# Cross-attention loop: maxima turned by VectorE, PSUM banks dealt anew, paired groups of narrow products

## What is computed

```python
x = x + tanh(g[0]) * long_convolution_mix(ctx, ctx, layernorm(x))
x = x + tanh(f[0]) * soft_expert_mix(layernorm(x))
x = x + tanh(g[1]) * L1_xattn(layernorm(x), ctx, ctx)
x = x + tanh(f[1]) * top2_of_8_experts(layernorm(x))

def L1_xattn(q, k, v):                 # b = 16, d = 256, m = n = 512
    h = 8                              # so heads of 32 channels
    qh, kh = q.reshape(b * h, 32, m), k.reshape(b * h, 32, n)
    vh = v.reshape(b * h, 32, n)
    qk = einsum('bdm,bdn->bmn', qh, kh) / sqrt(32)
    return einsum('bmn,bcn->bcm', softmax(qk, -1), vh)
```

## Time and profile before

| | us |
|---|---|
| times of three runs | 1622.12, 1619.13, 1624.82 |
| median | 1622.12 |
| span of the profiled execution (no other time is given for it) | 1622.8 |
| attention: from the first `stir` to the last group of values | 522.4 to 1031.1 |
| second products, first and last start | 543.9, 1028.0 |
| busy over the span: PE, weight loads, DVE, ACT, POOL | 94%, 66%, 73%, 60%, 64% |

### The profile page before, as it was taken

One profiled execution on the slowest core, in us unless ns is written; L12 is line 12 of the kernel. 1 busy time (PEld: TensorE's weight loads), 2 busy tenths in 40 slices (PEclk: granted clock), 3 DMA queues, 4 the chain that ended last, 5 costly groups with the idle time before them and its releaser, 6 DMA issues.

```text
span 1622.8 us, 28609 instructions
## 1 busy us (share of the span) xinstructions
PE 1524.7 (94%) x8929; PEld 1067.6 (66%) x8929; DVE 1189.2 (73%) x1868; ACT 981.3 (60%) x1529; POOL 1031.2 (64%) x855
## 2 busy tenths in 40 slices
PE   4999999998887999999999999888999999999996
PEld 3677777777554644444444444378999998999985
DVE  7788888888827777777777776275777777777774
ACT  6433333334724478888888877746777766766773
POOL 3788888885307588888888887502555555555553
PEclk8999999999998999999999999999999999999998
DMA  7344444445763967777776872581444444444443
GB/s 256 108 131 134 136 142 142 142 132 131 207 176 110 211 163 188 200 187 187 198 190 185 201 188 68 178 303 29 78 78 78 79 78 79 79 78 73 75 77 52
DMA packets 111131, 224.27 MB, mean 138 GB/s; under 512 B 12992, under 2 KB 12992, under 8 KB 110144
## 3 DMA queue, kind: packets, MB, share of 16 engines
q1 hardware_dynamic: 94560, 185.10, 40.3%
q0 software_dynamic: 15904, 37.23, 13.2%
q10 hardware_dynamic: 576, 0.79, 0.2%
HBM read 146.71 MB, written 75.84 MB: 137 GB/s over the span
## 4 chain that ended last, share of the span: by engine, by line
PE 33%; DMA 24%; issue 4%; DVE 4%; ACT 2%; POOL 1%; SPq 0%; ACTq 0%; POOLq 0%; DVEq 0%
DMA out_rows<-XN,slots 22%; PE pB L1471 10%; PE pO L1481 8%; PE pA L1453 7%; PE pO L1494 4%; PE pO L1645 1%; DMA XN<-normed_rows,slots 1%; PE pA L1633 1%; PE pB L1462 1%; PE pA L1549 1%; POOL out_rows L1435 1%; DVE low L1827 1%; DVE XN L2010 0%; DMA qs<-q_low 0%; DVE XN L1944 0%
## 5 line engine op out<-in xcount | busy, mean ns | idle before, releaser
L1827 DVE TENSOR_REDUCE low<-pA 128x2 f32<-128x1024 f32 x256 | 307.0, 1223 | 109.4 <-PE pA L1453 95.8
L1722 ACT ACTIVATE pt<-pB 128x512 f32<-128x512 f32 x512 | 287.7, 594 | 89.7 <-PE pB L1471 81.1
L1435 POOL DMA_INDIRECT out_rows<-XN,slots x71 | 196.9, 2773 | 217.9 <-DMA out_rows<-XN,slots 170.1
L436 PE MATMUL y<-kv,toep 128*128 128x288 f32 x1280 | 326.0, 411 | 9.0 <-DVEq L63 5.8
L436 PEld LDWEIGHTS y<-kv,toep 128*128 128x128 f32 x1280 | 238.0, 190 | 96.8 <-DVEq L63 34.0
L1633 PEld LDWEIGHTS pA<-XN,fc 128*128 128x128 f32 x2272 | 265.6, 192 | 10.9 <-issue 5.6
L1633 PE MATMUL pA<-XN,fc 128*128 128x128 f32 x2272 | 266.4, 276 | 5.0 <-DVE XN L1990 4.0
L1471 PE MATMUL pB<-qs,ks 98*128 98x512 f32 x512 | 226.9, 446 | 3.3 <-ACT pt L1722 2.4
L1471 PEld LDWEIGHTS pB<-qs,ks 98*128 98x128 f32 x512 | 95.6, 188 | 192.2 <-ACT pt L1722 149.2
L406 ACT ACTIVATE ym<-y 128x384 f32<-128x384 f32 (+1 forms) x128 | 52.6, 411 | 228.9 <-PE y L436 228.9
L1787 ACT ACTIVATE proj_high<-WP 128x2048 fp32r x71 | 135.7, 1912 | 83.6 <-PE pO L1645 83.6
(11 more groups left out here) (294 smaller groups left out, 2448.4 us busy)
## 6 DMA issues: line engine op xcount, KB each, us to landing
ks<-ctx_high SPq DMA_DIRECT2D x62, 256.0 KB, 4.6
qs<-q_high SPq DMA_DIRECT2D x62, 256.0 KB, 6.1
kc<-in_ctx_conv SPq DMA_DIRECT2D x32, 384.0 KB, 5.5
XN<-in_x SPq DMA_DIRECT2D x16, 512.0 KB, 9.8
toep<-kernel_and_skip SPq DMA_DIRECT2D x32, 256.0 KB, 3.5
ct<-in_ctx SPq DMA_DIRECT2D x16, 512.0 KB, 6.6
ctx_high<-kh SPq DMA_DIRECT2D x16, 512.0 KB, 4.5
ctx_low<-kl SPq DMA_DIRECT2D x16, 512.0 KB, 5.2
```

Of the source, the lines that this page charges most:

```text
L436: m = pe.matmul(y[half].rearrange("p (l n) c -> p l n c", l=CB)[:, l, :, 0:PAIRS], toep[u][:, (l - s) * P:(l - s + 1) * P], kv[u][:, half, ...
L1435: pool.indirect_dma_start(out=out["out"], out_offset=bass.IndirectOffsetOnAxis(ap=slots[:, j:j + 1], axis=0), in_=ys[j % 2], in_offset=Non ...
L1722: act.activation(pt[s][:, h, :], bank(u, n), ACT.Exp, scale=SCALE1).then_inc(s_exp, 1)
L1827: dve.tensor_reduce(ap(low[u % 2], t % CB * NH + t // CB, [[NH, 2], [1, 1]]), pA[n % 2], op=ALU.max, axis=AX.X, negate=True).then_inc(s_re ...
```

## The change

- **Maxima.** `halves` moves from POOL to DVE, after the last reduction of a unit (in beat 5, for unit `j + 1`), and a third operation there turns 128x32 in blocks of 32x32 into `turned`. `maxima` on PE, `keep` on ACT and the tensor `tops` are gone. `shift` is now four DMAs, one for each 32 queries of a block, each 32 pieces of 128 bytes (4 KB), instead of two of 8 KB in rows of 2 KB.
- **Banks.** `pB` has three banks and a second product waits for the exponential three places before it; `pO` has one, for values alone, so values 0 wait for `att` of the unit before. The sums of unit `j - 1` go into a bank of `pB` as place 7 of 17; the logarithm reads it and is counted with the exponentials, and the second product of beat 9 waits for it.
- **Groups.** Both groups of sums stand together at beat 7, and values 0 and 1 at beat 15; values 2 are at beat 3, values 3 at beat 11.
- **Order.** In beats 3, 6, 7, 8, 10, 11, 13, 14 and 15 the score stands before the second product (before: 2, 5, 10, 13). DVE refines after beat 3, measures after 7, scales after 11. ACT makes the high query after exponential 0, the norm after 4, the logarithm after 6, the inverse after 10, both roots after 15.
- The routing and expert stages get other names for the same number of banks.

```diff
-        low = [sb(st, f"low{i}", [P, CB, NH]) for i in range(2)]
-        split = sb(st, "split", [P, CB, 2 * NH])
+        low = [sb(st, f"low{i}", [P, NH * CB]) for i in range(2)]
+        split = sb(st, "split", [P, 2 * NH * CB])
+        turned = sb(st, "turned6", [P, SQUARE])
-        pB = [pb(st, f"pB{i}", [P, C]) for i in range(2)]
-        pO = [pb(st, f"pO{i}", [P, C]) for i in range(2)]
+        pB = [pb(st, f"pB{i}", [P, C]) for i in range(3)]
+        pO = pb(st, "pO", [P, C])
+        SHIFTS = 16 * P // HD1
+        SUM = 7
-        TURN = 10
+        EARLY_AT = (3, 6, 7, 8, 10, 11, 13, 14, 15)
             def shift(j, u):
-                sp.wait_ge(s_exp, made(j - 1, TURN) if not isinstance(j, int) or j > 0 else 1)
-                for row in range(2):
-                    part = tops[row * NH:(row + 1) * NH]
-                    sp.dma_start(qs[u][NS + row:NS + row + 1], bass.AP(part.tensor, part.offset, [list(part.ap[0]), [C, 1], [1, C]])).then_inc(s_md, 16)
+                sp.wait_ge(s_sp, 3 * j + 3)
+                for n in range(P // HD1):
+                    rows = qs[u][NS:NS + 2].rearrange("r h m -> r (h m)")
+                    sp.dma_start(ap(rows, n * HD1, [[P, NH * CB], [1, HD1]]),
+                                 ap(turned[n * SQUARE:(n + 1) * SQUARE], 0, [[HD1, 1], [1, HD1]])).then_inc(s_md, 16)
             def second(j, u, s, h):
-                n = place(j, s, h)
+                n = place(s, h)
                 if s == 0 and h == 0:
-                    pe.wait_ge(s_md, 32 * j + 32)
-                wait(pe, s_exp, made(j, n - 2))
-                pe.matmul(bank(u, n), ks[u][0:NS + 2, h, s * P:(s + 1) * P].bitcast(F32R), qs[u][0:NS + 2, h, :].bitcast(F32R),
+                    pe.wait_ge(s_md, SHIFTS * j + SHIFTS)
+                if n >= 3:
+                    pe.wait_ge(s_exp, made(j, n - 3))
+                elif exists(j - 1):
+                    pe.wait_ge(s_exp, made(j - 1, TILES - 1 + n % 2))
+                pe.matmul(pB[n % 3], ks[u][0:NS + 2, h, s * P:(s + 1) * P].bitcast(F32R), qs[u][0:NS + 2, h, :].bitcast(F32R),
                           start=True, stop=True).then_inc(s_b, 1)
             def values(j, i, u, s):
                 if s == 0:
                     pe.wait_ge(s_v[u], i * 16 + 16)
-                    wait(pe, s_ln, j)
+                    wait(pe, s_att, j)
+            def sums(j, to):
+                pe.wait_ge(s_add, 4 * j + 4)
+                pe.wait_ge(s_exp, made(j, place(CB - 1, NH - 1)))
+                for rows, last in ((part_sum, False), (pt[CB - 1], True)):
+                    for h in range(NH):
+                        m = pe.matmul(to[h * HD1:(h + 1) * HD1, :], ones, rows[:, h, :], start=not last, stop=last)
+                    m.then_inc(s_sum, 1)
             def body(j, i, u):
                 before = following(j, i, u, -1)
                 for beat in range(TILES):
-                    if beat in (2, 5, 13):
+                    if beat in EARLY_AT:
                         score(*ahead(j, i, u, beat))
-                    if beat == TURN and exists(j + 1):
+                    if beat == SUM and exists(j - 1):
+                        pe.wait_ge(s_exp, made(j, SUM - 3))
+                        sums(j - 1, pB[SUM % 3])
+                    second(j, u, beat // NH, beat % NH)
+                    if beat not in EARLY_AT:
                         score(*ahead(j, i, u, beat))
-                        wait(pe, s_exp, made(j, TURN - 2))
-                        maxima(j + 1, bank(u, TURN))
...
+                    if beat == 3 and exists(j - 1):
+                        values(*before, 2)
+                    if beat == 11 and exists(j - 1):
+                        values(*before, 3)
+                    if beat == 15:
                         values(j, i, u, 0)
-                    if beat == 15:
                         values(j, i, u, 1)
+            def halves(j, u):
+                dve.wait_ge(s_red, DUOS * j + DUOS)
+                dve.tensor_copy(split[:, 0:TILES].bitcast(F32R), low[u % 2]).then_inc(s_sp, 1)
+                dve.wait_ge(s_sp, 3 * j + 1)
+                dve.tensor_tensor(split[:, TILES:].bitcast(F32R), low[u % 2], split[:, 0:TILES], ALU.subtract).then_inc(s_sp, 1)
+                wait(dve, s_md, SHIFTS * j)
+                dve.sem_inc(s_go, 1)
+                dve.wait_ge(s_sp, 3 * j + 2)
+                dve.transpose(turned, split).then_inc(s_sp, 1)
```

More of the change, by code:

```diff
@@ L1190, in following, with place @@
             return j + n, i + (u + n) // TRIP, (u + n) % TRIP
[L1192 to L1198 removed]
+        def place(s, h):
+            return NH * s + h + (1 if NH * s + h >= SUM else 0)
         def made(j, n):
[L1202 removed]
+            if isinstance(j, int) and j == 0:
+                return n + 1 if n < SUM else n
+            return RING * j + n
         def wait(eng, signal, count):
@@ L1408, in _ @@
             rows_roots()
-            halves(0, 0)
             constants()
@@ L1477, in values @@
                     pe.wait_ge(s_v[u], i * 16 + 16)
-                    wait(pe, s_ln, j)
-                pe.wait_ge(s_exp, made(j, place(j, s, NH - 1)))
+                    wait(pe, s_att, j)
+                pe.wait_ge(s_exp, made(j, place(s, NH - 1)))
                 for h in range(NH):
-                    m = pe.matmul(pO[u % 2][h * HD1:(h + 1) * HD1, :], vt[u][:, s, h * HD1:(h + 1) * HD1], pt[s][:, h, :],
+                    m = pe.matmul(pO[h * HD1:(h + 1) * HD1, :], vt[u][:, s, h * HD1:(h + 1) * HD1], pt[s][:, h, :],
                                   start=(s == 0), stop=(s == CB - 1))
                 m.then_inc(s_av, 1)
-            def sums(j, u, last):
-                if last:
-                    pe.wait_ge(s_exp, made(j, place(j, CB - 1, NH - 1)))
-                else:
-                    pe.wait_ge(s_add, 4 * j + 4)
-                    wait(pe, s_att, j)
-                rows = pt[CB - 1] if last else part_sum
-                for h in range(NH):
-                    m = pe.matmul(pO[(u + 1) % 2][h * HD1:(h + 1) * HD1, :], ones, rows[:, h, :], start=not last, stop=last)
-                m.then_inc(s_sum, 1)
-            def finish(j, i, u, beat):
-                if beat == 2:
-                    values(j, i, u, 2)
-                if beat == 5:
-                    sums(j, u, False)
-                if beat == 7:
-                    sums(j, u, True)
-                if beat == 10:
-                    values(j, i, u, 3)
+            def sums(j, to):
[5 more added lines that the diff above has]
+                    m.then_inc(s_sum, 1)
             def body(j, i, u):
@@ L1510, in body @@
                 for beat in range(TILES):
-                    if beat in (2, 5, 13):
+                    if beat in EARLY_AT:
                         score(*ahead(j, i, u, beat))
-                    if beat == TURN and exists(j + 1):
-                        score(*ahead(j, i, u, beat))
-                        wait(pe, s_exp, made(j, TURN - 2))
-                        maxima(j + 1, bank(u, TURN))
-                    second(j, u, beat // NH, beat % NH)
-                    if beat not in (2, 5, TURN, 13):
-                        score(*ahead(j, i, u, beat))
-                    if exists(j - 1):
-                        finish(*before, beat)
-                    if beat == 13:
+                    if beat == SUM and exists(j - 1):
[3 more added lines that the diff above has]
+                    if beat not in EARLY_AT:
+                        score(*ahead(j, i, u, beat))
+                    if beat == 3 and exists(j - 1):
[3 more added lines that the diff above has]
+                    if beat == 15:
                         values(j, i, u, 0)
-                    if beat == 15:
                         values(j, i, u, 1)
-            idle = pO[0][:, C // 2:]
+            idle = pB[2][:, C // 2:]
             stir(pe, idle, 12)
@@ L1532, in _ @@
                     stir(pe, idle, 3)
-            maxima(0, pB[1])
             pe.wait_ge(s_one, 6)
@@ L1590, in _ @@
                 turn(n)
[L1591 to L1592 removed]
+            sums(UNITS - 1, pB[2])
             for q in range(QUADS):
@@ L1666, in _, with logarithm @@
             act.preload_act_table_set("natural_log_exp_and_others")
-            def keep(j, rows, count):
-                act.wait_ge(s_b, count)
-                if not isinstance(j, int) or j > 0:
-                    act.wait_ge(s_md, 32 * j)
-                act.activation(tops.bitcast(F32R), rows[0:2 * NH, :], ACT.Copy).then_inc(s_exp, 1)
-            def logarithm(j, u):
+            def logarithm(j, rows):
                 act.wait_ge(s_sum, 2 * j + 2)
                 wait(act, s_inv, j)
-                act.activation(lns, pO[(u + 1) % 2], ACT.Ln).then_inc(s_ln, 1)
+                act.activation(lns, rows, ACT.Ln).then_inc(s_exp, 1)
             def inverse(j):
-                act.wait_ge(s_ln, j + 1)
```

(3 more changed lines are left out.)

97 lines of the change are left out of this document (35 added, 62 removed).

## The result

| | before | after |
|---|---|---|
| median of four runs each, us | 1620.62 (1618.3 to 1624.82) | 1602.98 (1601.45 to 1606.12) |
| span of the profiled execution | 1622.8 | 1602.2 (time 1603.89) |
| first second product of unit 1, of unit 30 | 559.82, 1001.00 | 563.19, 984.64 |
| last sums | 1033.49 | 1015.11 |

What follows compares the result with a forecast made beforehand. TensorE's order bounds each 15.20 us unit; less 0.47 (turns) and 0.64 (pairs) gives 14.09, plus a 0.36 VectorE stall 14.45. Gains of 22.1 (29 units), 1.5 (start) and 1.0 (end) make 24.6: 1597.5 us, range 1585 to 1612.

Steps and rivals of the forecast that it cites:

- TensorE's order, 14.09 without stalls: Steady attention unit: TensorE's 15.20 us less 0.47 for the maxima's turns and 0.64 for two pairs of groups.
- c14: Beat 14's score on TensorE: wanted at 11.16 us of the unit, able to start at 11.52 after VectorE's jobs.
- The size of the stall, 0.36: Wait of beat 14's score for VectorE's reduction in each unit, making the period 14.45 us.
- halves 0.85: VectorE's new copy, subtraction and transpose cost 0.85 us a unit, within bounds of 0.5 and 1.45.
- Rival 1: VectorE's row fits without a stall: period 14.09 to 14.15, whole kernel 1588 us; chance 0.18.
- GpSimd loses halves, 1.2 to spare: GpSimd's additions end at 3.7 us of the next unit; the sums want them at 4.94.
- It waited 1.45 at 549.7 for loads, which stays.: First unit: TensorE's 1.45 us wait for loads was taken as unchanged.
- rival 3: The shift's small pieces land late, holding each unit's first second product: at 7 us landing, 1655 us; chance 0.08.
- After it 0.41 for the old shift, which goes.: First unit: a 0.41 us wait for the old shift disappears, part of 1.5 us gained there.
- The logarithm: ScalarE's logarithm delays beat 9's second product from 7.61 to 7.67 us; that 0.06 hides in the 0.36 stall.
- values 0 held by `att`: End of unit, one values bank: VectorE's scaling ends at 12.03 us, values 0 want 12.21 plus the stall, 0.5 to spare.
- rival 4: Nothing to be had: pairs cost a drain or ScalarE runs dry in them; period near 15.1, 1619 us; chance 0.05.

Runs made afterwards that it cites:

- Experiment 1: Changed kernel with the copy and two-input subtraction in VectorE's halves written as one-input reductions: 1589.95 us, ratio 0.9792, period 14.073.
- experiment 7: Experiment 1 plus four unused turns before beat 10's second product: 1625.76 us as plain fp32 products, 1605.51 us as transposes.
- experiment 6: Values 0 sent before the unit's last second product, undoing one pair: 1612.02 us on the changed kernel, 1599.73 us on Experiment 1.
- experiment 5: Experiment 1 plus an unused 128x512 reduction on VectorE behind the transpose in halves: 1610.17 us, period 14.714.
- experiment 4: Changed kernel with VectorE's refining moved from beat 3 to beat 15 of the unit before: 1603.97 us, ratio 0.9872.
- experiment 9: Experiment 1 plus 30 unused products of the identity on TensorE during the wait in unit 0: 1592.67 us, ratio 0.979.

## Why the prediction was right, and where not

- **TensorE's order, 14.09 without stalls: right.** Experiment 1 has 14.05 to 14.10 in every steady unit, 14.073 in the mean. Its terms hold one by one: 0.47 for the turns (0.44, experiment 7), 0.32 for a pair (0.32, experiment 6).
- **The place of the stall and who sets it: right in the main.** c14, charged to VectorE's reduction, VectorE without a gap, next to no slack (experiment 5). Not foreseen: some 0.2 of it is lost already at beat 10, and of the row's nine jobs those ahead of beat 5's score have their own cover (experiment 4).
- **The size of the stall, 0.36: near (0.48), but by luck, for the reason was not in the sum.** The failed step is "halves 0.85". It took the copy at its time alone, as the rows of the routing stage show it. Here `halves` is 0.76 undisturbed (experiment 1) and up to about 1.9 held, as GpSimd's `query_low` falls. By the row's true prices (refining 0.87 for 1.01, measuring 1.24 for 1.36, 0.09 of the way to the freed score not seen at all) there would have been no stall: two errors of opposite sign. Rival 1, the row fits, is what the same change does with other instructions in `halves`. Its 1588 for this case was measured at 1589.95.
- **GpSimd was costed for its own time only.** "GpSimd loses halves, 1.2 to spare" is right as far as it goes: the sums waited for it nowhere in the steady units. The step asked what GpSimd's jobs need and not what they run beside. The Trainium skill ("SBUF — State Buffer", Who interferes with whom) has the rule: VectorE and GpSimd share one pair of ports as an exclusive lock, which VectorE's copies and casts can take and which two operands in SBUF take against a GpSimd instruction that reads SBUF, while a reduction on this chip does not contend. By it the first to start keeps the pair for its whole instruction. No trace shows a port, but what the traces show agrees: the copy held up to 1.30 us, the subtraction up to 1.13, held only to the end of the piece under way when `query_low` is cut in four, the copy that started first (742.56) not held, and reductions never (0.169 to 0.171 us over 32 units in experiment 1).
- **The period's gain: 19.7 for 22.1.** The period is 14.53 for 14.45, and 29 x 0.08 are the 2.4.
- **The first unit: wrong, and the larger miss.** Forecast 1.5 us gained (its parts, 0.41, 0.47 and one pair of 0.32, make 1.2); measured 3.4 lost up to unit 1. 1.1 of that stands ahead of unit 0's first second product (545.07, before 543.93) and is hardly the change's: 0.5 ahead of the first `stir`, where nothing was changed (522.88, before 522.36), and 0.5 between it and the first score: 5.1 us for 4.6, and of the experiments seven have 5.1 there and four 4.5 to 4.6. The other 2.2 came in unit 0 (18.12 from its first second product to unit 1's, before 15.89). Two steps failed.
  - "It waited 1.45 at 549.7 for loads, which stays." Of SyncE only the steady unit was worked out, where four issues for two had 0.5 us to spare, and this held: no steady unit waits for the shift (rival 3). In unit 0 the load of unit 2 stands behind the shift on the queue. The shift's issues took 2.77 us instead of 1.38, the load's last issue moved from 542.63 to 544.22, and the wait grew by 1.5.
  - "After it 0.41 for the old shift, which goes." It did not go, it grew. Unit 1's shift is now issued right behind unit 3's loads and the query's stores, and landed at 562.65 where the old one landed at 559.77: 2.9 later. In experiment 4, which starts like the changed kernel, TensorE stood 2.14 us waiting for it, as its timeline shows:

```profile
561.12 0.50 PE L1456 MATMUL pB<-qs,ks 98*128 98x512 f32 x1 [2.14 <-DMA qs<-turned]
```

The forecast had 4.61 us for this landing; it took 9.8 in the changed kernel and 9.5 in experiment 4. So rival 3 came true, but in the first unit only. The small pieces alone don't do that, since in the steady units they land in 1.75; what the traffic beside them does and what its place on the queue does was not separated.
- **What the lower clock cost in the first units: little here.** Behind the pause of 2.95 us products followed each other at 0.43 us until the pair of values was through (3.64 for 1.92). But of the changed kernel's time it can have cost no more than 0.5 us: the shift landed at 562.65, and the product that needed it came at 563.19. Experiment 1 shows the same behind its pause of 2.38 us, with a clock of 0.52 from 560 to 567, and there it stood behind the shift and cost 3.1 (experiment 9).
- **The end: 2.0 for 1.0**, where GpSimd's additions set the time as said; the first of the last unit start at 1005.34, 17.1 before's. Another **2.2 us** came behind the last sums, in stages costed at nothing (587.1 from there to the end, before 589.3). Only bank names differ there. The experiments, with the changed kernel's code in those stages, take from 586.3 to 590.7, so the 2.2 are no more than what one execution differs by from another.
- **The logarithm: forecast 0.06 late, hidden in the stall: right.** The load at 817.86 waits 0.26 for it, and the score behind comes 0.08 late. It does so in experiment 1 as well, where it is part of the 14.073; in the changed kernel c14 follows, at a time that VectorE sets, and covers it.
- **ScalarE dry in the pairs, values 0 held by `att`** (rival 4 and a stated cover): not seen in the steady units.
- **The point, 1597.5.** It was taken from the first three times, median 1622.12; with the fourth the kernel before has 1620.62. So of the 7.0 us by which the gain fell short only 5.5 show in the point. (Its "0.7 above the median" sets a span against times, which are 1.7 to 1.8 longer than their spans; the forecast gain does not hang on it.)

## What to carry to other kernels

When a small job is moved to VectorE, look at what GpSimd runs at that moment, not only at how long either takes alone: a 0.17 us copy became up to 1.3 us here, in a row with under 0.1 us of slack, and cost some 13 us over the kernel. Writing it and the subtraction with one-input reductions gave the 13 back, cutting GpSimd's instruction into four pieces 9. Before shortening such a row, look where it really begins: 0.87 us taken out ahead of a wait bought nothing. And work out the first round of a pipeline by itself: two more DMA issues that fit easily in the steady round stood there ahead of the load that TensorE was waiting for, and the next shift landed 9.8 us after its last issue where it takes 1.75 in the steady round.

## What the runs showed of the hardware that was not expected

- VectorE's 128x16 copy and subtraction end 0.02 to 0.04 us after the GpSimd instruction they run beside: 0.17 us alone, up to 1.30 and 1.13. A one-input reduction of the same size beside the same instruction: 0.17.
- Turns by plain products of fp32 are twice the work of `transpose`: eight records and 1.15 us a unit, against four and 0.44.
- A pause of 2.95 us (2.38 in experiment 1, 1.45 before) in the first units, with work at full clock ahead of it, was followed by a stretch mostly at the 1.2 GHz level: 553 to 563 in the changed kernel, 560 to 567 in experiment 1, 551 to 553 before.
- Pieces of 128 bytes from SBUF to SBUF, 128 in a unit (17088 packets under 512 B over the kernel, 12992 before), delayed nothing in the steady units: they land 1.75 us after the last issue, the old rows of 2 KB took 1.85. So of the two rules that the prediction sets side by side the one on copies within SBUF fits. What they cost was SyncE's time to issue them, 0.61 to 0.66 us for each of four (0.58 to 0.62 for each of two before).
